# One core, eight sublayers: the dispatch multiply of a soft mixture of experts, and the square and key copies of an attention, change engines

## The chip, the core and the metric

The program runs on one core of a Trainium2 chip. The core has five engines that run their own instruction queues in order: PE (TensorE), DVE (VectorE), ACT (ScalarE), POOL (GpSimd) and SP (SyncE, which here only starts DMAs). They meet through semaphores. The metric is the device time of one launch in microseconds; the kernel before was run three times, and the profiled execution is the fastest of them.

## The reference

Eight sublayers over a residual stream `x` of 16 x 256 tokens of 128 numbers, each `x = x + layernorm(f(layernorm(x)))`. The change touches two of them. The soft mixture of experts, with 64 experts of 32 slots:

```
logits = einsum('bmd,dnp->bmnp', x, phi)        # b 16, m 256, 64*32 slots
dispatch = softmax(logits, axis=0)              # over the batches
combine = softmax(logits over all slots)
slots = einsum('bmd,bmnp->bnpd', x, dispatch)
y = einsum('bnpd,nde->bnpe', slots, W) + b
out = einsum('bnpd,bmnp->bmd', y, combine)
```

and the attention at the end of the seventh sublayer, with 16 query heads and 4 key heads of 8 numbers:

```
q, k, v = n @ q_w, n @ k_w, n @ v_w             # 128 + 32 + 32 columns
q, k = rms_norm(q), rms_norm(k)                 # per head, over 8 numbers
q, k = rope(q) * q_gain, rope(k)
k, v = repeat(k, 4), repeat(v, 4)               # a key head for 4 query heads
```

## The kernel before

All intermediate data stay in SBUF; the program goes from sublayer to sublayer. Each engine has a program of its own, made of Python generators; `together` advances the generators of several lanes in rounds, lane n one or more rounds behind lane n-1, so the order of an engine's queue is that of the rounds.

**Soft mixture of experts.** The 2048 slots go in 16 passes ("halves" `h` in the code) of 128 slots. The tokens of a batch are two tiles of 128, `mt` 0 and 1. For each pass and tile, `L3` holds the logits as 128 partitions by 16 batches by 128 slots (2048 columns) and `D3` the dispatch weights of the same shape. Two chains of buffers alternate. In one call of `dve_half`, DVE works on the fronts of pass h and finishes pass h-1:

- `dve_front(mt)`: the maximum over the batches by a tree of tensor_tensor instructions of 1024, 512 and 256 columns (L2051) and a last one (L2054), then the subtraction (L2064), the maximum over slots (L2065) and small updates.
- `dve_weights(mt)`: after ACT's exponential (L1966), the sum over the batches by the same tree, its reciprocal `m1` (L2083), and for tile 0 the multiply of `D3` by `m1` (L2086), 128x2048. This is the dispatch weight.
- then, for pass h-1, `dve_ya` four times (L2107: adds an expert product in psum to the output in SBUF) with `dve_eT3` between (L306: a copy from psum).

For tile 1 the same multiply is POOL's (`pool_half`, L2137), followed in its queue by the small sums `ls` (L2143, L2145). PE uses the product in `pe_slots` of the next half. PE's order is: logits of tile 1, slots, transposes and experts, then the products `pe_po` (L1929) with transposes and the next logits (L1870) between. ACT copies from psum (L302), takes the exponentials (L1966, L1975) and hands on the transposed outputs that the first L1929 of a half waits for; these copies stand in its queue behind the exponential of tile 1.

**Last attention.** 8 groups of 512 tokens in two runs of 4 lanes, one round apart. In each lane PE makes 192 columns of query, key and value for each token (L1262), ACT scales them out of psum into `QK` (L1712, L1713) and squares the 640 columns of queries and keys (L1718), DVE sums over each head (L1617), ACT takes the root of the mean plus epsilon (L1721), DVE inverts (L1620), applies the gain (L1623), scales (L1628) and turns by the position (L1636 to L1640). POOL writes each key head four times into `KR` (L1760, four copies of 128x128). PE transposes queries and then `KR` (`pe_tr4`, L294), DVE makes the masked queries from psum (L1562), ACT the masked keys (L1568). PE's attention matmuls (L389 and on) stand behind the last lane's transposes in its queue.

Of the kernel before, what the change touches and what calls it, by code (L numbers as in the profile page):

```python
# [10 lines left out]
ALU = mybir.AluOpType  # L11
# [6 lines left out]
LANES = 4  # L18
# [142 lines left out]
def build(nc, tables, wa, wb, wc, wd, wm, wi, ve, co, step, frame, xin, out):  # L161
    ctx = ExitStack()
    with ctx:
# [39 lines left out]

        ident = wv("ident")
        XG = [XA[:, 4 * g:4 * g + 4, :] for g in range(8)]
        mhalf, mone, epsc = MISC[:, 0:4], MISC[:, 212:216], MISC[:, 216:217]
        WI_S = wCs[:, 0:1152].bitcast(I32)
        WGU = wCs[:, 1152:2304]
        STEPM = wCs[:, 2304:2688]
# [134 lines left out]
        def idle(n):  # L344
            for _ in range(n):
                yield
# [861 lines left out]
        def pe_mid(pe, c, g):  # L1208
            v = views23(c)
            XT = v["XT"]  # L1210
            k = (("l2", g // 4), c.n)
            pe.wait_ge(A4, (("l2", g // 4), 2 * c.n + 1, "on"))
            pe_tok(pe, c, k, wv("l2o"), XT, 0, c.A, "y")
            pe.wait_ge(GD[LANES], "folded")
            yield
            yield
            k = (g, "l2f")
            pe.wait_ge(c.D, (k, "normed", 3))
            pe_tr4(pe, c, k, v["XN"], 0, c.A)
            yield  # L1220
            pe.wait_ge(c.A, (k, "xT"))
            yield from pe_mlp(pe, c, k, XT, wv("l2w1"), 4, w3("l2w2"), v["h3"], c.D, c.A)
            yield
            yield
            k = (g, "l3m")
            pe.wait_ge(c.D, (k, "mixed"))
            pe_tr4(pe, c, k, v["Z"], 0, c.A)
            yield
            k = (g, "l3n")
            pe.wait_ge(c.D, (k, "normed", 3))  # L1230
            pe_tr4(pe, c, k, v["YN"], 1, c.A)
            yield
            pe.wait_ge(c.A, (k, "xT"))
            pe.wait_ge(AD[LANES], "taps")
            for n in range(2):
                ps = c.bank(pe, n, c.A, (k, "val_silu", n))
                pe.e.matmul(ps[:, :], tap_weights(3, n), v["NT"], start=True, stop=False)
                for s in (1, 2, 3):
                    for b in range(0, 512, 256):
                        ins = pe.e.matmul(ps[:, b + s:b + 256], tap_weights(3 - s, n), v["NT"][:, b:b + 256 - s],  # L1240
                                          start=False, stop=s == 3 and b == 256)
                ins.then_inc(*c.P.inc((k, "val", n)))
            yield
            for n in range(2):
                ps = c.bank(pe, n, c.A, (k, "gated", n))
                pe.e.matmul(ps[:, :], wv("inp")[:, 256 + 128 * n:384 + 128 * n], v["NT"], start=True, stop=True).then_inc(
                    *c.P.inc((k, "gate", n)))
            yield
            for b in range(2):
                yield from pe_scan(pe, c, (g, "scan", b), b, v, (g, "l3n"), (g, "l3m"))  # L1250
            yield from pe_relu_mlp(pe, c, (g, "mm"), v, "mfc", "mpj")
            yield
            k = (("l3", g // 4), c.n)
            pe.wait_ge(c.D, ((g, "am"), "mixed"))
            pe_tr4(pe, c, k, v["Z"], 0, c.A)
            yield
            pe.wait_ge(c.A, (k, "xT"))
            for g2 in range(2):
                ps = c.bank(pe, g2, c.A, (k, g2, "qkv"))
                for j in range(2):  # L1260
                    t = 2 * g2 + j
                    ins = pe.e.matmul(ps[:, j * 192:(j + 1) * 192], XT[:, t * 128:(t + 1) * 128], wv("qkv"),  # L1262
                                      start=True, stop=True)
                ins.then_inc(*c.P.inc((k, g2, "qkv_pe")))
            yield
            yield
            yield
            pe.wait_ge(c.D, (k, "roped"))
            pe_tr4(pe, c, k, v["QK"][:, :, 0:128], 0, c.D, "qa")
            pe.wait_ge(c.G, (k, "repeated"))  # L1270
            pe_tr4(pe, c, k, v["KR"], 1, c.A, "ka")
            yield

# [307 lines left out]
        def dve_mid(dve, c, g):  # L1581
# [31 lines left out]
            yield  # L1613
            yield
            rb, sq, un = v["rb"], v["sq"], v["un"]
            dve.wait_ge(c.A, (k, "qk_sq"))
            dve.e.tensor_reduce(rb, sq.rearrange("p t (h d) -> p (t h) d", d=8), X_AX, ALU.add).then_inc(*c.D.inc((k, "ms")))  # L1617
            yield
            dve.wait_ge(c.A, (k, "rms"))
            dve.e.reciprocal(rb, rb).then_inc(*c.D.inc())  # L1620
# [16 lines left out]
            dve.e.tensor_tensor(u8[:, :, :, 0:4], q8[:, :, :, 4:8], turn("sin8", 0, 4), ALU.mult)  # L1637
            dve.e.tensor_tensor(u8[:, :, :, 4:8], q8[:, :, :, 0:4], turn("sin8", 4, 4), ALU.mult).then_inc(*c.D.inc())
            dve.wait_ge(c.D)
            dve.e.tensor_tensor(QK, sq, un, ALU.add).then_inc(*c.D.inc((k, "roped")))  # L1640
            yield
            dve_queries(dve, c, k, v, "mq", "qa_tr")
            yield
# [24 lines left out]
        def act_mid(act, c, g):  # L1668
# [45 lines left out]
                        "p (j d) -> p j d", d=8).unsqueeze(2).to_broadcast([128, 4, 4, 8]), ACT.Identity, scale=rs)  # L1714
                ins.then_inc(*c.A.inc((k, g2, "qkv")))
            ended([c.A], (k, "vp"))
            act.wait_ge(c.A, (k, 1, "qkv"))
            act.e.activation(v["sq"], QK, ACT.Square).then_inc(*c.A.inc((k, "qk_sq")))  # L1718
            yield
            act.wait_ge(c.D, (k, "ms"))  # L1720
            act.e.activation(v["rb"], v["rb"], ACT.Sqrt, scale=0.125, bias=epsc).then_inc(*c.A.inc((k, "rms")))  # L1721
            yield
            yield
            act_keys(act, c, k, v, "mk", "ka_tr")
# [13 lines left out]
        def pool_mid(pool, c, g):  # L1738
            yield from pool_norm(pool, c, (g, "l2ap"))
            yield from pool_norm(pool, c, (g, "l2f"))  # L1740
            yield from idle(3)
            yield from pool_norm(pool, c, (g, "l2fp"))
            yield from pool_norm(pool, c, (g, "l3x"))
            pool_mean_square(pool, c, (g, "l3n"), mhalf)
            yield
            v = views23(c)
            yield from idle(3)
            for b in range(2):
                yield from pool_scan(pool, c, (g, "scan", b), b, v, (g, "l3n"))
            pool_mean_square(pool, c, (g, "mm"), mone)  # L1750
            yield from idle(3)
            k = (("l3", g // 4), c.n)
            yield
            pool_mean_square(pool, c, k, mhalf)
            yield from idle(3)
            pool.wait_ge(c.D, (k, "roped"))
            for t in range(4):
                kr4 = v["KR"][:, t, :].rearrange("p (g r d) -> p g r d", g=4, d=8)
                k3_ = v["QK"][:, t, 128:160].rearrange("p (g d) -> p g d", d=8)
                ins = pool.e.tensor_copy(kr4, k3_.unsqueeze(2).to_broadcast([128, 4, 4, 8]))  # L1760
            ins.then_inc(*c.G.inc((k, "repeated")))
            yield from idle(2)

        def pool_fold(pool):

# [108 lines left out]
        def pe_slots(pe, banks, c, q):  # L1874
            k = ("smoe", q)
            for mt in range(2):
                D3 = views2(c, mt)["D3"]
                if mt == 0:
                    pe.wait_ge(c.D, (k, "disp"))
                else:  # L1880
                    pe.wait_ge(c.G, (k, 1, "disp"))
                for g in range(4):
                    if mt == 0:
                        banks.fill(pe, g, c.A, (k, "SL", g))
                    for i in range(4):
                        ins = pe.e.matmul(psum[g][:, i * 128:(i + 1) * 128], XN4[:, 4 * g + i, mt, :], D3[:, 4 * g + i, :],
                                          start=mt == 0 and i == 0, stop=mt == 1 and i == 3)
                    if mt == 1:
                        ins.then_inc(*c.P.inc((k, "slots", g)))
# [166 lines left out]
        def dve_front(dve, c, other, q, mt):  # L2056
# [1 line left out]
            tm, al, mr, m1 = v["tm"], v["al"], MR[:, mt, :], v["m1"]  # L2058
            dve.wait_ge(c.A, (k, mt, "L", 3))
            if q:  # L2060
                dve.wait_ge(other.G, (before, 1, "disp")) if mt else dve.wait_ge(other.D, (before, "disp"))
            dve_over_batches(dve, c, v["L3"], v["D3"], m1, ALU.max)
            dve.wait_ge(c.D)
            dve.e.tensor_tensor(v["D3"], v["L3"], v["mb"], ALU.subtract).then_inc(*c.D.inc((k, mt, "D")))  # L2064
# [13 lines left out]
        def dve_weights(dve, c, q, mt):  # L2078
            k, v = ("smoe", q), views2(c, mt)
            dve.wait_ge(c.A, (k, mt, "Dexp"))  # L2080
            dve_over_batches(dve, c, v["D3"], v["SL"], v["m1"], ALU.add)
            dve.wait_ge(c.D)
            dve.e.reciprocal(v["m1"], v["m1"]).then_inc(*c.D.inc((k, mt, "m1")))  # L2083
            if mt == 0:
                dve.wait_ge(c.D, (k, mt, "m1"))
                dve.e.tensor_tensor(v["D3"][:, 0:16, :], v["D3"][:, 0:16, :], v["mb"][:, 0:16, :],  # L2086
                                    ALU.mult).then_inc(*c.D.inc((k, "disp")))

        def dve_eT3(dve, c, q):
            for n in range(2):  # L2090
# [41 lines left out]

        def pool_half(pool, cs, h):
            c, other, k = cs[h % 2], cs[(h - 1) % 2], ("smoe", h)
            v = views2(c, 1)
            pool.wait_ge(c.D, (k, 1, "m1"))
            pool.e.tensor_tensor(v["D3"], v["D3"], v["mb"], ALU.mult).then_inc(*c.G.inc((k, 1, "disp")))  # L2137
            for mt in range(2):
                v, ls = views2(c, mt), LS[:, mt, :]
                pool.wait_ge(c.A, (k, mt, "E"))  # L2140
# [390 lines left out]

        def dve_program(e):
            dve = Engine(e)
            dve.e.memset(epsc, EPS).then_inc(*DD[LANES].inc("epsc"))
            dve.e.memset(mone, -1.0).then_inc(*DD[LANES].inc("mone"))
            dve.e.memset(mhalf, -0.5).then_inc(*DD[LANES].inc("mhalf"))
            dve.wait_dma(got_wi)
# [286 lines left out]
```

## Time and profile before

| | us |
|---|---|
| three runs, median (lowest, highest) | 3416.62 (3413.53, 3418.79) |
| the profiled execution, its own time | 3413.53 |
| its span in the trace | 3411.4 |
| PE busy, of the span | 2832.5 (83%) |
| DVE busy | 2209.4 (65%) |
| ACT busy | 1850.9 (54%) |
| POOL busy | 406.3 (12%) |
| mean granted clock of PE | 0.913 of full |
| the 16 passes of the mixture of experts, about | 1190 to 1820 |
| end of the two runs of query and key work | 2298 and 2930 |

The span is the time between the first and the last instruction of the program. Busy time is not time on the path that sets the end: only the chain of waits and the idle times, stretch by stretch, tell that.

### The profile page before, as it was taken

The numbers are of one execution on the slowest core, as the hardware profiler recorded it, in microseconds if no ns is written. First come the engines' busy times: TensorE is split into PE (matmuls) and PEld (weight loads), VectorE is DVE, ScalarE is ACT, GpSimd is POOL, SyncE is SP. The second block draws the span as 40 slices with busy tenths as digits, with TensorE's granted clock in tenths as the row PEclk, the third lists the DMA queues.
The fourth block names the chain that finished last, engine by engine and source line by source line (L and its number), as shares of the span: only waits on it lengthen the run. The fifth ranks groups of instructions, "written<-read, shape, count | busy, mean of one in ns | idle before, by whom it ended". The sixth has DMA issues, their size and how long they took to land.

```text
span 3411.4 us, 75794 instructions
## 1 busy us (share of the span) xinstructions
PE 2832.5 (83%) x31896; PEld 2260.7 (66%) x31896; DVE 2209.4 (65%) x5927; ACT 1850.9 (54%) x4115; POOL 406.3 (12%) x551
## 2 busy tenths in 40 slices
PE   5788888788888668888886889978887999786995
PEld 3566666556666568777785767867666787675574
DVE  4766656676656589899996663476565545755437
ACT  3566665566666578878783443354444434543332
POOL 1210101210001111111111011120100211002000
PEclk7899999899989889999997999988999999797997
DMA  2000000000000000000001000010100001001000
GB/s 96 1 2 1 2 1 1 1 1 2 14 1 14 29 7 7 7 7 7 7 1 63 3 14 13 1 50 3 39 15 3 25 2 38 14 3 50 1 1 26
DMA packets 16996, 48.95 MB, mean 14 GB/s; under 512 B 1168, under 2 KB 9616, under 8 KB 14096
## 3 DMA queue, kind: packets, MB, share of 16 engines
q1 hardware_dynamic: 16656, 44.10, 3.7%
q8 instruction: 252, 4.13, 0.5%
q14 instruction: 88, 0.72, 0.1%
HBM read 41.99 MB, written 2.10 MB: 13 GB/s over the span
## 4 chain that ended last, share of the span: by engine, by line
PE 54%; DVE 32%; ACT 10%; issue 2%; POOL 1%; DMA 0%; DVEq 0%; SPq 0%; POOLq 0%; ACTq 0%
PE ps L329 8%; PE ps L320 5%; PE ps L1358 3%; DVE LN L2051 3%; PE ps L1929 3%; PE ps L386 3%; PE ps L473 3%; DVE M L489 2%; DVE RS L239 2%; DVE LN L2064 2%; PE ps L1369 2%; PE ps L294 2%; PE ps L1870 2%; PE ps L754 2%; DVE M L633 1%
## 5 line engine op out<-in xcount | busy, mean ns | idle before, releaser
L302 ACT COPY LN<-ps 128x512 f32<-128x512 f32 (+4 forms) x560 | 284.9, 550 | 265.8 <-PE ps L772 59.5
L281 POOL TENSOR_TENSOR RS<-RS,MISC 128x4 f32<-128x4 f32 x184 | 189.1, 1028 | 1458.8 <-DVE RS L263 779.4
L489 DVE TENSOR_REDUCE M<-ps 128x6 f32<-128x768 f32 x256 | 241.6, 954 | 135.8 <-PE ps L473 95.5
L294 PE MATMUL ps<-cons,LN 128*128 128x128 f32 x672 | 125.3, 322 | 155.5 <-ACT LN L268 57.0
L386 PE MATMUL ps<-LN 32*128 32x256 f32 x1024 | 186.3, 438 | 55.2 <-DVE LN L525 31.6
L294 PEld LDWEIGHTS ps<-cons,LN 128*128 128x128 f32 x672 | 88.5, 163 | 200.0 <-ACT LN L268 55.0
L320 PE MATMUL ps<-LN,wAB 128*128 128x512 f32 x384 | 202.2, 658 | 19.4 <-DVE LN L959 18.1
L633 DVE TENSOR_REDUCE M<-ps 128x12 f32<-128x1536 f32 x64 | 112.4, 1756 | 146.5 <-PE ps L376 146.5
L389 PE MATMUL ps<-LN 32*128 32x256 f32 x1024 | 201.8, 473 | 2.2 <-DVE M L489 2.2
L1975 ACT ACTIVATE LN<-LN,RS 128x128 f32<-128x128 f32 x512 | 199.0, 404 | 1.6 <-DVE RS L2076 0.6
L549 ACT ACTIVATE LN<-ps 128x768 f32<-128x768 f32 x128 | 103.7, 810 | 168.2 <-PE ps L473 133.7
L329 PE MATMUL ps<-wAB,LN 128*128 128x128 f32 x1536 | 185.9, 280 | 7.1 <-DVE LN L1517 5.2
L329 PEld LDWEIGHTS ps<-wAB,LN 128*128 128x128 f32 x1536 | 179.4, 195 | 17.7 <-DVE LN L1517 9.1
L1929 PE MATMUL ps<-LN,wAB 128*128 128x128 f32 x1024 | 136.8, 291 | 44.1 <-ACT LN L302 43.6
L2051 DVE TENSOR_TENSOR LN<-LN 128x1024 f32<-128x1024 f32 (+2 forms) x192 | 150.7, 785 | 26.8 <-ACT LN L302 16.1
L539 ACT ACTIVATE LN<-ps 128x768 f32<-128x768 f32 x128 | 103.8, 811 | 112.9 <-PE ps L376 94.0
L1929 PEld LDWEIGHTS ps<-LN,wAB 128*128 128x128 f32 x1024 | 129.5, 205 | 48.0 <-ACT LN L302 47.1
L268 ACT ACTIVATE LN<-LN,RS 128x128 f32<-128x128 f32 x256 | 105.5, 488 | 76.4 <-POOL RS L275 75.3
L1870 PE MATMUL ps<-wAB,LN 128*128 128x128 f32 x1024 | 126.2, 281 | 22.3 <-ACT LN L302 21.0
L386 PEld LDWEIGHTS ps<-LN 32*128 32x128 f32 x1024 | 82.5, 190 | 92.1 <-issue 39.0
L1870 PEld LDWEIGHTS ps<-wAB,LN 128*128 128x128 f32 x1024 | 122.4, 198 | 22.8 <-ACT LN L302 21.2
L376 PE MATMUL ps<-cons 32*128 32x64 bf16 x6144 | 135.4, 193 | 0.3
(362 smaller groups left out, 7321.3 us busy)
## 6 DMA issues: line engine op xcount, KB each, us to landing
LN<-frame SPq DMA_DIRECT2D x16, 1024.0 KB, 5.0
wAB<-wb SPq DMA_DIRECT2D x16, 256.0 KB, 2.6
LN<-frame SPq DMA_DIRECT2D x8, 512.0 KB, 3.6
LN<-wd SPq DMA_DIRECT2D x8, 512.0 KB, 6.9
wAB<-wa SPq DMA_DIRECT2D x1, 3840.0 KB, 15.9
wCs<-wc SPq DMA_DIRECT2D x1, 2336.0 KB, 8.3
XA<-xin SPq DMA_DIRECT2D x8, 256.0 KB, 7.6
y<-XA SPq DMA_DIRECT2D x8, 256.0 KB, 2.3
```

What stands on the lines that cost most here:

```text
L281: pool.e.tensor_tensor(c.r[:, 40:44], c.r[:, 36:40], mhalf, ALU.pow).then_inc(*c.G.inc((k, "rstd")))
L294: ins = pe.e.transpose(ps[:, n * 128:(n + 1) * 128], src[:, n, :], ident)
L302: act.e.copy(dst, ps).then_inc(*c.A.inc(named(k, done)))
L320: pe.e.matmul(ps[:, :], w1[:, j * 128:(j + 1) * 128], xT, start=True, stop=True).then_inc(*c.P.inc((k, "up", j)))
L329: ins = pe.e.matmul(ps[:, t * 128:(t + 1) * 128], h3[:, j, t * 128:(t + 1) * 128], w2[:, j, :], start=j == 0, stop=j == nh - 1)
L386: pe.e.matmul(psum[n][:, 0:256], qt.ka[rows[j], o:o + 128], qt.qa[rows[j], o:o + 256], start=True, stop=False)
L389: pe.e.matmul(psum[n][:, 128:384], qs.qa[rows[j], o + 128:o + 256], qs.ka[rows[j], o:o + 256], start=True, stop=False)
L489: return dve.e.tensor_reduce(cols[:, 2 - 2 * h:4 - 2 * h, :, q.at], src, X_AX, ALU.max, negate=True)
L1870: ins = pe.e.matmul(psum[4 + g][:, i * 128:(i + 1) * 128], XTA[:, t * 128:(t + 1) * 128], phi[:, q * 128:(q + 1) * 128], start=True, stop= ...
L1929: ins = pe.e.matmul(psum[2 * gp + n][:, i * 128:(i + 1) * 128], eTb[2 * gp + n][:, i * 128:(i + 1) * 128], v["ym"][:, 4 * g + i, :], start ...
L1975: ins = act.e.activation(v["L3"][:, b, :], v["L3"][:, b, :], ACT.Exp, bias=v["nm"][:, b:b + 1], accum_out=v["rs"][:, b:b + 1])
L2051: dve.e.tensor_tensor(dst, src[:, 0:n, :], src[:, n:2 * n, :], op).then_inc(*c.D.inc())
```

## The change

In the mixture of experts, DVE's multiply for tile 0 goes to POOL: POOL's queue now has both multiplies of a pass, each released by the reciprocal of its tile, ahead of the `ls` sums. PE and DVE wait for POOL's count in place of DVE's. In the last attention, ACT's square becomes a DVE tensor_tensor, the factor 1/8 and epsilon move from ACT's square root into a DVE tensor_scalar ahead of it, and POOL's four copies of the keys become DVE copies behind the turn; the event "roped" comes after them, so the transposes of the queries wait for the copies too. The constant `epsc` and its memset go.

```diff
@@ pe_mid
             pe.wait_ge(c.D, (k, "roped"))
             pe_tr4(pe, c, k, v["QK"][:, :, 0:128], 0, c.D, "qa")
-            pe.wait_ge(c.G, (k, "repeated"))
             pe_tr4(pe, c, k, v["KR"], 1, c.A, "ka")
@@ dve_mid
-            dve.wait_ge(c.A, (k, "qk_sq"))
-            dve.e.tensor_reduce(rb, sq.rearrange(...), X_AX, ALU.add).then_inc(*c.D.inc((k, "ms")))
+            dve.wait_ge(c.A, (k, 1, "qkv"))
+            dve.e.tensor_tensor(sq, QK, QK, ALU.mult).then_inc(*c.D.inc())
+            dve.wait_ge(c.D)
+            dve.e.tensor_reduce(rb, sq.rearrange(...), X_AX, ALU.add).then_inc(*c.D.inc())
+            dve.wait_ge(c.D)
+            dve.e.tensor_scalar(rb, rb, 0.125, EPS, ALU.mult, ALU.add).then_inc(*c.D.inc((k, "ms")))
...
-            dve.e.tensor_tensor(QK, sq, un, ALU.add).then_inc(*c.D.inc((k, "roped")))
+            dve.e.tensor_tensor(QK, sq, un, ALU.add).then_inc(*c.D.inc())
+            dve.wait_ge(c.D)
+            for t in range(4):
+                kr4 = v["KR"][:, t, :].rearrange("p (g r d) -> p g r d", g=4, d=8)
+                k3_ = QK[:, t, 128:160].rearrange("p (g d) -> p g d", d=8)
+                ins = dve.e.tensor_copy(kr4, k3_.unsqueeze(2).to_broadcast([128, 4, 4, 8]))
+            ins.then_inc(*c.D.inc((k, "roped")))
@@ act_mid
-            act.wait_ge(c.A, (k, 1, "qkv"))
-            act.e.activation(v["sq"], QK, ACT.Square).then_inc(*c.A.inc((k, "qk_sq")))
...
-            act.e.activation(v["rb"], v["rb"], ACT.Sqrt, scale=0.125, bias=epsc).then_inc(*c.A.inc((k, "rms")))
+            act.e.activation(v["rb"], v["rb"], ACT.Sqrt).then_inc(*c.A.inc((k, "rms")))
@@ pool_mid: the wait for "roped" and the four tensor_copy into KR go
@@ pe_slots
-                if mt == 0:
-                    pe.wait_ge(c.D, (k, "disp"))
-                else:
-                    pe.wait_ge(c.G, (k, 1, "disp"))
+                pe.wait_ge(c.G, (k, mt, "disp"))
@@ dve_front
-                dve.wait_ge(other.G, (before, 1, "disp")) if mt else dve.wait_ge(other.D, (before, "disp"))
+                dve.wait_ge(other.G, (before, mt, "disp"))
@@ dve_weights
             dve.e.reciprocal(v["m1"], v["m1"]).then_inc(*c.D.inc((k, mt, "m1")))
-            if mt == 0:
-                dve.wait_ge(c.D, (k, mt, "m1"))
-                dve.e.tensor_tensor(v["D3"][:, 0:16, :], v["D3"][:, 0:16, :], v["mb"][:, 0:16, :],
-                                    ALU.mult).then_inc(*c.D.inc((k, "disp")))
@@ pool_half
-            v = views2(c, 1)
-            pool.wait_ge(c.D, (k, 1, "m1"))
-            pool.e.tensor_tensor(v["D3"], v["D3"], v["mb"], ALU.mult).then_inc(*c.G.inc((k, 1, "disp")))
+            for mt in range(2):
+                v = views2(c, mt)
+                pool.wait_ge(c.D, (k, mt, "m1"))
+                pool.e.tensor_tensor(v["D3"], v["D3"], v["mb"], ALU.mult).then_inc(*c.G.inc((k, mt, "disp")))
```

## Rows read from the trace of the kernel before

**Rows 1.** The page, part 1: busy us, share of the span, instructions.

```profile
PE 2832.5 (83%) x31896; PEld 2260.7 (66%) x31896; DVE 2209.4 (65%) x5927; ACT 1850.9 (54%) x4115; POOL 406.3 (12%) x551
```

**Rows 2.** The chain of waits from 1180 to 1850 us, shares by line.

```profile
by line: DVE LN L2051 16.8%; PE ps L1929 15.8%; DVE LN L2064 10.6%; PE ps L1870 8.4%; DVE LN L2086 5.5%; DVE RS L2065 4.9%; ACT LN L1966 4.9%; ACT LN L1975 4.4%; PE ps L1899 3.3%; DVE LN L2107 2.9%; ACT LN L302 2.5%; DVE M L2083 2.3%; issue
```

**Rows 3.** The two multiplies by line: ns least/median/most, first and last start.

```profile
L2086 DVE TENSOR_TENSOR LN<-LN,M x16: 2291/2292/2293, 1201.9 to 1767.1; 128x2048 f32<-128x2048 f32 x16
...
L2137 POOL TENSOR_TENSOR LN<-LN,M x16: 4535/4562/4580, 1215.7 to 1781.4; 128x2048 f32<-128x2048 f32 x16
```

**Rows 4.** Timeline of one half: start us, us, instruction, [idle before <-releaser].

```profile
1691.88 2.29 DVE L2086 TENSOR_TENSOR LN<-LN,M 128x2048 f32<-128x2048 f32 x1
...
1694.27 2.41 DVE L2051 TENSOR_TENSOR LN<-LN 128x1024 f32<-128x1024 f32 x3
...
1699.36 1.91 ACT L1966 ACTIVATE LN<-LN 128x2048 f32<-128x2048 f32 x1 [3.21 <-DVE LN L2064]
...
1702.77 2.83 PE L1929 MATMUL ps<-LN,wAB 128*128 128x128 f32 x16 [3.73 <-ACT LN L302]
...
1705.11 0.95 DVE L2083 RECIPROCAL M<-M 128x128 f32<-128x128 f32 x1
...
1706.14 4.58 POOL L2137 TENSOR_TENSOR LN<-LN,M 128x2048 f32<-128x2048 f32 x1 [23.27 <-DVE M L2083]
```

**Rows 5.** Timeline, instructions by line and chain where DVE and POOL overlap.

```profile
1215.74 4.54 POOL L2137 TENSOR_TENSOR LN<-LN,M 128x2048 f32<-128x2048 f32 x1 [36.23 <-DVE M L2083]
...
L2051 DVE TENSOR_TENSOR LN<-LN x1: 2064/2064/2064, 1219.3 to 1219.3; 128x1024 f32<-128x1024 f32 x1
...
1694.27 1.24 DVE LN L2051
...
1259.97 2.29 DVE L2064 TENSOR_TENSOR LN<-LN,M 128x2048 f32<-128x2048 f32 x1
1260.19 2.15 POOL L2145 TENSOR_TENSOR MISC<-MISC,RS 128x16 f32<-128x16 f32 x1
...
L2145 POOL TENSOR_TENSOR MISC<-MISC,RS x30: 218/222/2145, 1251.1 to 1791.6; 128x16 f32<-128x16 f32 x30
```

**Rows 6.** Chain at two halves; busy us by engine in one stretch, then PE's granted clock.

```profile
1552.68 2.05 PE ps L1929 x16
...
1557.39 1.79 PE ps L1870 x16
...
1709.13 1.79 PE ps L1870 x16
...
1702.70:1709.00 6.30, 6.23 (x41) 6.23 (x42) 5.92 (x16) 6.30 (x27) 2.86 (x1) 0.73 0.01 3
```

**Rows 7.** Last attention: PE, PEld, DVE, ACT, POOL busy by stretch; timeline, first run.

```profile
2273.00:2298.20 25.20, 9.91 (x36) 7.29 (x36) 22.78 (x38) 16.57 (x42) 4.99 (x15) 0.59 0.04 15
2905.30:2930.50 25.20, 9.77 (x36) 7.29 (x37) 22.77 (x38) 16.57 (x42) 4.99 (x15) 0.64 0.04 17
...
2269.92 1.13 DVE L1525 SCALAR_TENSOR_TENSOR LN<-ps,RS,LN 128x128 f32<-128x128 f32 x4 [3.35 <-PE ps L329]
...
2276.48 0.82 DVE L1640 TENSOR_TENSOR LN<-wAB,LN 128x640 f32<-128x640 f32 x1
...
2278.52 1.41 DVE L1562 TENSOR_SCALAR LN<-ps,cons 128x512 f32<-128x512 f32 x2 [0.48 <-PE ps L294]
...
2285.72 1.41 DVE L1562 TENSOR_SCALAR LN<-ps,cons 128x512 f32<-128x512 f32 x2 [0.86 <-PE ps L294]
...
2298.20 2.18 PE L294 MATMUL ps<-cons,LN 128*128 128x128 f32 x8 [4.63 <-DVE LN L1640]
2298.21 1.00 POOL L1760 COPY LN<-LN 128x128 f32<-128x128 f32 x4 [5.81 <-DVE LN L1640]
```

**Rows 8.** Groups of instructions by form: count, busy us, mean ns, idle before.

```profile
L824 DVE TENSOR_SCALAR LN<-LN 128x256 f32<-128x256 f32 x32 | 8.9, 278 | 0.0
...
L2075 DVE COPY MISC<-RS 128x16 f32<-128x16 f32 x32 | 5.6, 175 | 1.1
```

More of the change, by code:

```diff
@@ L205, in build @@
         XG = [XA[:, 4 * g:4 * g + 4, :] for g in range(8)]
-        mhalf, mone, epsc = MISC[:, 0:4], MISC[:, 212:216], MISC[:, 216:217]
+        mhalf, mone = MISC[:, 0:4], MISC[:, 212:216]
         WI_S = wCs[:, 0:1152].bitcast(I32)
@@ L1615, in dve_mid @@
             rb, sq, un = v["rb"], v["sq"], v["un"]
-            dve.wait_ge(c.A, (k, "qk_sq"))
-            dve.e.tensor_reduce(rb, sq.rearrange("p t (h d) -> p (t h) d", d=8), X_AX, ALU.add).then_inc(*c.D.inc((k, "ms")))
+            dve.wait_ge(c.A, (k, 1, "qkv"))
+            dve.e.tensor_tensor(sq, QK, QK, ALU.mult).then_inc(*c.D.inc())
+            dve.wait_ge(c.D)
+            dve.e.tensor_reduce(rb, sq.rearrange("p t (h d) -> p (t h) d", d=8), X_AX, ALU.add).then_inc(*c.D.inc())
+            dve.wait_ge(c.D)
+            dve.e.tensor_scalar(rb, rb, 0.125, EPS, ALU.mult, ALU.add).then_inc(*c.D.inc((k, "ms")))
             yield
@@ L1754, in pool_mid @@
             pool_mean_square(pool, c, k, mhalf)
[L1755 to L1762, printed above, removed]
+            yield from idle(5)
         def pool_fold(pool):
@@ L2533, in dve_program @@
             dve = Engine(e)
-            dve.e.memset(epsc, EPS).then_inc(*DD[LANES].inc("epsc"))
             dve.e.memset(mone, -1.0).then_inc(*DD[LANES].inc("mone"))
```

## The prediction

> **What bounds the kernel now.** I read the page first for the engines' shares, then the chain of waits over the soft mixture-of-experts stretch (1180 to 1850 us), where two thirds of the edits' instructions lie, then the timeline of one half of that stretch and of the end of the last attention's preparation, and last every place where a POOL instruction and a DVE instruction with two SBUF inputs overlap. The reader is to see four things.
>
> The page [rows 1] shows PE at 83% and DVE at 65% of the span, and says nothing of which one sets the end of a stage. The chain does: in the mixture-of-experts stretch the largest part is DVE's halving tree L2051, and L2086, the multiply that the change moves, holds 5.5% of it [rows 2]; 5.5% of 670 us is 36.9 us, which is all 16 instructions of 2.29 us [rows 3]. So each of the 16 halves waits for this multiply. The timeline says why [rows 4]: behind it on DVE stands the second tile's tree (L2051) and subtraction, and for that ACT (idle 3.21 us) and then PE (idle 3.73 us) wait.
>
> POOL is almost empty (12%) [rows 1], and does the same multiply for the second tile in 4.56 us [rows 3]. While it does so there, DVE works on psum (the `ya` updates and the `eT` copies), not on two SBUF tensors.
>
> **The mixture of experts, part by part (16 halves).** Removed from DVE: L2086. From its start to the start of the next L2051 are 1694.27 - 1691.88 = 2.39 us [rows 4]. The next L2051 now follows the reciprocal with the gap that it had behind L2086, 0.09 us, so the plain gain on the chain is 2.30 us in each half, 36.8 us in all. ACT and PE idle longer than that at this place, so nothing else would eat it.
>
> Added to POOL: one 4.56 us multiply per half, released by the same reciprocal. POOL starts such a multiply 0.08 us after the reciprocal ends (1705.11 + 0.95 against 1706.14) [rows 4]. DVE's L2051 comes 0.09 us after it. The two therefore start together in every half, both reading two SBUF tensors, which in the kernel before happens at no half but by accident once. That accident is what I go by [rows 5]: POOL's multiply ran from 1215.74 to 1220.28, L2051 started at 1219.30 inside it and took 2.06 us instead of 1.24. It ended at 1221.36, so its 1.24 us of work fit behind 1220.12: it stood still for 0.82 of the 0.98 us that the two shared, until 0.16 us before POOL's end. The reverse is there too: POOL's 16-column L2145, 0.22 us as a rule, began 0.22 us into DVE's L2064 and lasted 2.15 us, until 0.08 us after L2064 was done. An instruction of one engine holds up the other's for as long as it reads.
>
> The Trainium skill states this as a rule (SBUF — State Buffer, section "Who interferes with whom"): a DVE instruction with two SBUF inputs and a GpSimd instruction that reads SBUF exclude each other for the whole instruction, and the first to start decides who waits. By it the multiply would block for all of its 4.56 us, an estimate of 0.15 us a half, or 2.4 us in all, above what I take from the rows; it is the rule that speaks against this change. The trace agrees with it but for those last 0.16 us: 0.82 of 0.98 us lost [rows 5].
>
> With the rows: reciprocal ends at 1691.84, POOL starts at 1691.92, has read out 4.56 - 0.16 = 4.40 us later at 1696.32, and only then does L2051 run, which before started at 1694.27. That is 2.05 us later instead of 2.30 earlier. If DVE is the first by a hair, its 1024-column L2051 (1.24 us) runs, POOL's multiply goes next in the gap behind it, and the 512-column one waits: 0.09 + 1.24 + 4.4 = 5.73 us after the reciprocal against 0.04 + 2.39 + 1.24 = 3.67 before, again 2.06. Who wins doesn't matter. L2051 is on the chain in all 16 halves, so 16 x 2.05 = **33 us later**. Bounds: if the loser still creeps (0.16 us of work in 0.98 us of overlap) it does 0.7 us of its work meanwhile and the loss is 1.3 us a half, 21 us; if POOL holds to its very end and starts first, 2.2 us, 35.
>
> What waits for POOL is covered: PE needs both products only for the slot matmuls in the next half, and the front of the next half needs them later still. Behind the new multiply in POOL's queue stand the second multiply, whose reciprocal comes 13 us later, and the small `ls` updates. No DMA and no queue issue is moved.
>
> Clock of PE: PE idles 3.73 us ahead of the first product matmuls (L1929). From that start to the next logits are 1557.39 - 1552.68 = 4.71 us in one half, and 1709.13 - 1702.77 = 6.36 us in the half of [rows 4], where the same instructions fall partly under a granted clock of 1.2 GHz (mean share 0.73) [rows 4, 6]. Along the chain seven halves look like the first and the rest like the second or worse. The idle time grows to 5.8 us, which does not speak for a better clock. I take +3 us in all; bounds 0 and seven halves turned, 7 x 1.65 = 12.
>
> **The last attention's queries and keys, 4 lanes in each of two runs.** ACT loses one pass over 640 columns a lane; DVE gains a product of 128x640 (nearest row L1640, 0.82 us), a small scale-and-add on 80 columns and four copies of 128x128. Nearest rows for these: a copy of 16 columns takes 0.175 us, a tensor_scalar of 256 columns 0.278 [rows 8]; I take 0.19 for the small one with its wait and 0.20 for a copy, 0.83 for the four with their wait (0.6 to 1.2 as bounds). POOL loses the four copies, 1.00 us.
>
> From 2273.0 to 2298.2 DVE is busy for 22.78 of 25.2 us, the second run likewise [rows 7]: turning of lane 0, sum of lane 1, queries of lane 0, turning of lane 1, and so on. PE's transposes wait for the last DVE turn (L1640), and the attention's first matmuls stand behind those in PE's queue. So what DVE is given here is on the path, and what ACT gives up isn't: in the new order DVE is late and ACT waits for it. Four turnings gain 0.83 each, 3.3 us. Three sums gain 0.82 + 0.04 + 0.19 = 1.05 each, 3.15 us; the first lane's comes before DVE's idle stretch of 3.35 us, where it waits for PE [rows 7], and costs nothing. Against that, DVE has idle gaps for PE ahead of three of the queries (0.48, 0.86 and 0.48 us again; the first two in [rows 7]), which the added work fills: 1.8 us. POOL's copies ran beside the transposes of the queries (1.00 us beside 2.18 us, both from 2298.20) so their removal saves nothing at the end. 3.3 + 3.15 - 1.8 = 4.65 us a run, **9.3 us** for both; with the bounds of the copies 7.5 to 12, and 6 if half of the sums find more cover. If the cover of the three gaps is gone it is 13.
>
> The removed memset and the scale and bias of the square root change nothing that can be seen.
>
> **Sum.** 33 + 9.3 + 3 = 45.3 us, against the profiled execution's 3413.5 us (span 3411.4 and 2.1 around it): 3458.8. That execution is the fastest of three and 3.1 us under their median, so 3462 for a median.
>
> **Rivals.** (a) DVE keeps ahead. If L2051 gets the port first and its followers, 0.02 us apart, keep it, or if the block is a thing of the one overlap, POOL's multiply runs in the shadow and the 36.8 us are gained: 3416.6 - 36.8 + 9.3 = 3389 us. The point from which this decides is a stall of L2051 under 1.7 us a half ((36.8 - 9.3) / 16). For it: DVE's gaps are 0.02 us, and only one L2051 was seen waiting. Against it: L2145 got in right behind L2064 although DVE had more to do. 1 in 10.
> (b) The port is shared rather than locked, or the creeping of [rows 5] holds: 21 + 9.3 = 30 us, 3447; or the attention's part is hidden and only the stall counts, 33 us, 3450. 1 in 7, and inside the range.
> (c) The clock falls in the seven good halves as well, and copies cost 0.3 us each: 35 + 13 + 12 = 60 us, 3477. 1 in 14.
> (d) Everything cancels: a stall of some 1.7 us. 1 in 50.
>
> **How the numbers follow.** The forecast has two chances in three; with (b) and (c) 88 in 100 end slower. Its own range is 3452 to 3472; with the bounds and with (b) and (c) 3438 to 3482, which leaves out (a), (d) and a little more. What a measurement can tell from no change here is 0.2%, 7 us. Faster 0.10, same 0.02, slower 0.88.
>
> **What would show it.** In the profile after, every POOL multiply of the first tile begins within 0.1 us of a reciprocal; the L2051 beside it (1024 or 512 columns) takes 4.4 us longer than elsewhere; halves are 2 us longer each; ACT's and PE's idle time ahead of the exponential and of L1929 grows by 2 us. In the attention, DVE from 2273 on takes some 5 us more until the last turn. Wrong would be: L2051 at its 1.24 us (then rival a, and the multiply on POOL would show the wait or none at all); stalls in which each takes part of the other's time; or attention halves that end when they did.

## The result and the profile after

The median went from 3417.7 us (3413.53 to 3426.17, 4 runs) to 3473.0 us (3470.69 to 3478.71, 4 runs): a ratio of 1.0166, 95% interval 1.0149 to 1.0183, so 55.3 us slower. The forecast was 3462 within 3438 to 3482, slower. The profiled execution took 3474.84 us, with a span of 3473.0, 61.6 us more than the span before.

The page, part 1, of the kernel after:

```profile
span 3473.0 us, 75794 instructions
PE 2850.8 (82%) x31896; PEld 2280.3 (66%) x31896; DVE 2255.4 (65%) x5958; ACT 1846.9 (53%) x4107; POOL 473.9 (14%) x535
```

Against [rows 1], DVE gave away 16 multiplies of 2.29 us, 36.7 us, and is busy 46.0 us longer, although the attention gave it under 14 us of new instructions. An instruction that stands still counts as busy, so that is the first sign of a stall. PE is busy 18.3 us longer with as many instructions, at a mean granted clock of 0.905 where it was 0.913.

All rows below are of the kernel after unless said otherwise. Its line numbers are lower than before's: the tree is L2048 (was L2051), the subtraction L2061 (L2064), the reciprocal L2080 (L2083), POOL's multiply L2131 (L2137), the exponential L1963 (L1966), the products L1926 (L1929).

The timeline of one half, start us, us, instruction, idle before and its releaser (before: [rows 4]):

```profile
1736.29 4.55 POOL L2131 TENSOR_TENSOR LN<-LN,M 128x2048 f32<-128x2048 f32 x1 [9.11 <-DVE M L2080]
1736.31 6.78 DVE L2048 TENSOR_TENSOR LN<-LN 128x1024 f32<-128x1024 f32 x3
...
1745.78 1.91 ACT L1963 ACTIVATE LN<-LN 128x2048 f32<-128x2048 f32 x1 [5.26 <-DVE LN L2061]
...
1749.19 3.78 PE L1926 MATMUL ps<-LN,wAB 128*128 128x128 f32 x16 [5.77 <-ACT LN L302]
```

POOL and DVE leave the reciprocal together. POOL's multiply takes its usual time and the three tree instructions take 6.78 us instead of 2.41. ACT now idles 5.26 us ahead of the exponential instead of 3.21, and PE 5.77 us ahead of the products instead of 3.73: 2.05 and 2.04 us more.

The chain of waits through the same half, in order of time, and then the busy times of that stretch by engine with PE's granted clock behind them (before: [rows 6]):

```profile
1736.31 5.61 DVE LN L2048
...
1745.78 1.91 ACT LN L1963
...
1749.19 3.78 PE ps L1926 x16
1752.97 1.71 PE ps L1896 x8
1754.68 2.09 PE ps L1926 x16
1756.77 1.34 PE ps L1870 x12
...
1749.20:1756.80 7.60, 7.60 (x42) 7.60 (x43) 6.00 (x17) 7.48 (x33) 4.25 (x1) 0.61 0.01 2
```

The stalled tree instruction is on the chain, with 5.61 us. And the 40 matmuls and transposes from the first products to the next logits take 1756.77 - 1749.19 = 7.58 us, where [rows 6] has 4.71 in a good half and the prediction 6.36 in a bad one. The granted clock of that stretch was 0.61, so most of it ran at 1.2 GHz, and PE had idled 5.77 us before it.

The subtraction by line, ns least/median/most, first and last start; the tree's 1024-column form and the products by form, busy us, mean ns of one, idle us before. First after:

```profile
L2061 DVE TENSOR_TENSOR LN<-LN,M x32: 2291/2292/2293, 1196.8 to 1825.3; 128x2048 f32<-128x2048 f32 x32
...
L2048 DVE TENSOR_TENSOR LN<-LN 128x1024 f32<-128x1024 f32 x64 | 144.6, 2259 | 22.6 <-ACT LN L302 16.1 <-ACT LN L1963 0.8
...
L1926 PE MATMUL ps<-LN,wAB 128*128 128x128 f32 x1024 | 151.2, 310 | 74.9 <-ACT LN L302 74.4 <-DVE wAB L306 0.5
```

and the same of the kernel before:

```profile
L2064 DVE TENSOR_TENSOR LN<-LN,M x32: 2291/2292/2294, 1193.2 to 1772.3; 128x2048 f32<-128x2048 f32 x32
...
L2051 DVE TENSOR_TENSOR LN<-LN 128x1024 f32<-128x1024 f32 x64 | 79.2, 1238 | 22.4 <-ACT LN L302 16.1 <-ACT LN L1966 0.8
...
L1929 PE MATMUL ps<-LN,wAB 128*128 128x128 f32 x1024 | 136.8, 291 | 44.1 <-ACT LN L302 43.6 <-DVE wAB L306 0.5
```

The tree's 64 large instructions take 65.4 us more; that is 15 of them at 5.60 us (the sixteenth collision fell otherwise, below). From the first subtraction to the last the mixture of experts takes 628.5 us instead of 579.1. The two stretches start 3.6 us apart already. That start differs by up to 6.7 us between the traces of this document, although nothing of either edit but a memset lies before it, so it is not put to the change.

To see where in a half the time went I cut each one at four events and added up over the halves in each trace (us; 16 intervals in the first column, 15 in the next two, 14 in the last):

| kernel | subtraction of tile 0 to that of tile 1 | to the first products | first to third products | to the next subtraction |
|---|---|---|---|---|
| before | 227.7 | 86.0 | 109.2 | 152.0 |
| after | 260.2 | 86.0 | 127.3 | 152.3 |

All of it is in two places: 32.5 us in the interval that holds the stall, and 18.1 us in the stretch from the first products to the third, which is PE alone and where nothing was added. In single halves that stretch takes 6.34 us at full clock. Before, six of 15 halves had that and the rest mostly 7.98 (one 9.18); after, one half has 6.34 and nine have 8.7 to 9.3. The granted clock of the stretch goes with it: 1.00 at 6.34 us, 0.79 at 7.98, 0.67 to 0.68 at 9.2. The last half is shorter in every kernel: 6.20 before, 7.43 after, and 4.55 in experiment 4.

The attention, DVE in the first run (before: [rows 7]), with the first reciprocal and the first attention matmul as its marks:

```profile
2326.87 0.65 DVE L1623 RECIPROCAL wAB<-wAB 128x80 f32<-128x80 f32 x1
...
2331.19 0.63 DVE L1648 COPY LN<-LN 128x128 f32<-128x128 f32 x4
2331.74 0.82 DVE L1616 TENSOR_TENSOR wAB<-LN 128x640 f32<-128x640 f32 x1
...
2333.45 0.20 DVE L1620 TENSOR_SCALAR wAB<-wAB 128x80 f32<-128x80 f32 x1
...
2355.91 1.97 PE L294 MATMUL ps<-cons,LN 128*128 128x128 f32 x8 [6.04 <-DVE LN L1648]
...
2357.81 1.22 PE L389 MATMUL ps<-LN 32*128 32x256 f32 x4
```

and of the kernel before the same marks, with PE's wait for POOL's copies between them:

```profile
2273.02 0.65 DVE L1620 RECIPROCAL wAB<-wAB 128x80 f32<-128x80 f32 x1
...
2299.27 0.72 PEld L294 LDWEIGHTS ps<-cons,LN 128*128 128x128 f32 x4 [0.35 <-POOL LN L1760]
...
2300.32 1.22 PE L389 MATMUL ps<-LN 32*128 32x256 f32 x4
```

From mark to mark: 30.94 us after, 27.30 before, 3.64 us more; the second run gives 3.64 as well. Together 7.3 us. PE waits for DVE's copies now (6.04 us idle). The sum for the profiled execution is 32.5 + 18.1 + 7.3 = 57.9 us, and 3.6 from the later start: 61.5 of 61.6.

### The profile page after: what moved, and what is told of

Its sections match the earlier page's. It is cut to its first block, busy times and chain, and to the rows that moved or that the text cites. A ratio compares the mean times of both kernels' runs of the same rounds, so it can differ in the third digit from the quotient of the medians.

```text
span 3473.0 us, 75794 instructions
## 1 busy us (share of the span) xinstructions
PE 2850.8 (82%) x31896; PEld 2280.3 (66%) x31896; DVE 2255.4 (65%) x5958; ACT 1846.9 (53%) x4107; POOL 473.9 (14%) x535
## 4 chain that ended last, share of the span: by engine, by line
PE 54%; DVE 33%; ACT 9%; issue 2%; POOL 1%; DMA 0%; DVEq 0%; SPq 0%; POOLq 0%; ACTq 0%
PE ps L329 7%; DVE LN L2048 5%; PE ps L320 5%; PE ps L1926 3%; PE ps L1357 3%; PE ps L386 3%; PE ps L473 3%; DVE M L489 2%; DVE RS L239 2%; DVE LN L2061 2%; PE ps L1368 2%; PE ps L294 2%; PE ps L1870 2%; PE ps L754 2%; ACT LN L302 1%
## 5 line engine op out<-in xcount | busy, mean ns | idle before, releaser
L2048 DVE TENSOR_TENSOR LN<-LN 128x1024 f32<-128x1024 f32 (+2 forms) x192 | 220.3, 1147 | 27.0 <-ACT LN L302 16.1
L1926 PE MATMUL ps<-LN,wAB 128*128 128x128 f32 x1024 | 151.2, 310 | 74.9 <-ACT LN L302 74.4
L1926 PEld LDWEIGHTS ps<-LN,wAB 128*128 128x128 f32 x1024 | 143.9, 225 | 78.8 <-ACT LN L302 78.0
L2131 POOL TENSOR_TENSOR LN<-LN,M 128x2048 f32<-128x2048 f32 x32 | 146.3, 4570 | 356.5 <-DVE M L2080 356.5
L329 PEld LDWEIGHTS ps<-wAB,LN 128*128 128x128 f32 x1536 | 179.4, 195 | 17.7 <-DVE LN L1516 9.1
L2100 DVE SCALAR_TENSOR_TENSOR LN<-LN,RS,ps 128x128 f32<-128x128 f32 x448 | 119.1, 339 | 34.3 <-PE ps L1926 34.3
```

Source lines behind the costliest of these rows:

```text
L329: ins = pe.e.matmul(ps[:, t * 128:(t + 1) * 128], h3[:, j, t * 128:(t + 1) * 128], w2[:, j, :], start=j == 0, stop=j == nh - 1)
L1926: ins = pe.e.matmul(psum[2 * gp + n][:, i * 128:(i + 1) * 128], eTb[2 * gp + n][:, i * 128:(i + 1) * 128], v["ym"][:, 4 * g + i, :], start ...
L2048: dve.e.tensor_tensor(dst, src[:, 0:n, :], src[:, n:2 * n, :], op).then_inc(*c.D.inc())
```

## The experiments

**1. The mixture-of-experts edit alone.** The diff's hunks of `pe_slots`, `dve_front`, `dve_weights` and `pool_half`; the attention as before.

> Only the mixture-of-experts edit, the attention as before. My theory (POOL's reading multiply shuts DVE's two-SBUF instructions out, and the delay then lets PE's clock fall): the 16 halves keep all of their 50 us (16 x 2.05 stall, some 18 from the clock), so about 3467 us, ratio 1.015; the 1024-column tree instruction beside POOL's multiply takes 5.6 us. Rival (the two edits make each other worse): under 40 us.

Measured: 3461.5 us (3461.16 to 3466.98) against 3417.9, ratio 1.0131 (1.0117 to 1.0144), 43.6 us. A half in its timeline:

```profile
1610.15 4.55 POOL L2131 TENSOR_TENSOR LN<-LN,M 128x2048 f32<-128x2048 f32 x1 [9.05 <-DVE M L2080]
1610.18 6.80 DVE L2048 TENSOR_TENSOR LN<-LN 128x1024 f32<-128x1024 f32 x3
...
1623.07 3.78 PE L1926 MATMUL ps<-LN,wAB 128*128 128x128 f32 x16 [5.79 <-ACT LN L302]
```

The same stall and the same slow products as with the whole change: first to last subtraction 628.6 us against 579.1, so the stretch holds the 50 us that were expected, while the medians show 43.6. By the medians four fifths of the loss are this edit's.

**2. The attention edit alone.**

> Only the attention edit, the multiply on DVE as before. My theory: 3.7 to 3.9 us in each of the two runs of lanes, 7.5 us in all, ratio 1.0022, and nothing elsewhere. Rival (the 3.5 us that the changed kernel is already behind ahead of the mixture of experts belong to the edit): 11 us.

Measured: 3424.3 us (3416.06 to 3438.87, 10 runs), ratio 1.0020 (1.0005 to 1.0034), 6.5 us. Its marks:

```profile
2272.64 0.65 DVE L1623 RECIPROCAL wAB<-wAB 128x80 f32<-128x80 f32 x1
...
2303.58 1.22 PE L389 MATMUL ps<-LN 32*128 32x256 f32 x4
```

30.94 us, the same 3.64 us a run more as with the whole change. In the stretches the two edits add up; by the medians they make 43.6 + 6.5 = 50.1 of 55.3 us, with some 5 us of uncertainty in each.

**3. The delay without POOL.** The kernel before, with one more DVE instruction behind the multiply that lasts about as long as the net delay of a half, 2.05 us (its result is used nowhere):

```diff
                                     ALU.mult).then_inc(*c.D.inc((k, "disp")))
+                dve.wait_ge(c.D, (k, "disp"))
+                dve.e.tensor_tensor(v["SL"][:, 0:14, :], v["D3"][:, 0:14, :], v["D3"][:, 0:14, :],
+                                    ALU.add).then_inc(*c.D.inc())
```

> The kernel before with one more DVE instruction of 1792 columns behind the multiply of tile 0 (it adds two copies of data into a scratch buffer and changes no result): the same 2.05 us of delay in each half, with POOL left alone. If the rest of the loss is PE's clock, as I hold, the halves come out as in the changed kernel: about 50 us, the time from the first products to the third ones at 8.5 us on average instead of 7.4, all L2051 at 1.24 us. If instead POOL and DVE cost more in other places (rival), this kernel loses only 33 us.

Measured: 3471.6 us (3466.13 to 3476.23), ratio 1.0156 (1.0140 to 1.0171). One half, the subtraction by line and the products by form:

```profile
1618.05 2.03 DVE L2089 TENSOR_TENSOR LN<-LN 128x1792 f32<-128x1792 f32 x1
...
1620.18 2.41 DVE L2051 TENSOR_TENSOR LN<-LN 128x1024 f32<-128x1024 f32 x3
...
L2064 DVE TENSOR_TENSOR LN<-LN,M x32: 2291/2291/2296, 1199.2 to 1827.7; 128x2048 f32<-128x2048 f32 x32
...
L1929 PE MATMUL ps<-LN,wAB 128*128 128x128 f32 x1024 | 151.2, 311 | 74.8 <-ACT LN L302 74.3 <-DVE wAB L306 0.5
```

The tree takes its 2.41 us, POOL is left as it was, and the stretch is 628.5 us all the same, with the products at 311 ns and the first-to-third stretches adding up to 127.0 us. So the 18 us on PE come with the delay alone; they need nothing of POOL's. The medians of experiments 1 and 3 are 10 us apart although this stretch is the same to 0.1 us: in the profiles 5.5 us of that lie ahead of the mixture of experts (first subtraction at 1193.6 and 1199.2) and 3.5 behind it, where the two kernels do not differ. A difference of a few microseconds between medians of two kernels is not evidence here; the stretches are.

**4. POOL does both multiplies, but later.** Experiment 1 with the first multiply released by the second tile's reciprocal, when DVE goes on to instructions that read psum:

```diff
-                pool.wait_ge(c.D, (k, mt, "m1"))
+                pool.wait_ge(c.D, (k, 1, "m1"))
```

> The mixture-of-experts edit alone, but POOL begins both multiplies only after the second tile's reciprocal, when DVE works on psum for about 10 to 12 us; they take 9.1 us. My theory: no overlap with a two-SBUF instruction of DVE, every tree instruction of 1024 columns at 1.24 us, 2.3 us gained in each half, 37 us, and up to 15 more because PE's idle time falls to 1.4 us and its clock holds: 3365 to 3380 us, ratio 0.985 to 0.989. Rival 1 (POOL's load itself costs time, wherever it lies): no gain. Rival 2 (the multiplies run into the next half's tree): gain shrinks by the overlap, seen as tree instructions above 1.24 us.

Measured: 3373.6 us (3370.92 to 3376.86), ratio 0.9870 (0.9857 to 0.9884): 44.3 us faster than before, and 99 faster than the change, which has the attention's 7 us as well. A half of it, the granted clock of a stretch, and the subtraction by line:

```profile
1596.27 2.41 DVE L2048 TENSOR_TENSOR LN<-LN 128x1024 f32<-128x1024 f32 x3
...
1604.78 2.05 PE L1926 MATMUL ps<-LN,wAB 128*128 128x128 f32 x16 [1.40 <-ACT LN L302]
...
1608.15 9.09 POOL L2131 TENSOR_TENSOR LN<-LN,M 128x2048 f32<-128x2048 f32 x2 [20.95 <-DVE M L2080]
...
1604.80:1609.30 4.50, 4.50 (x40) 4.50 (x41) 4.36 (x11) 4.50 (x17) 1.15 (x1) 1.00 0.00 0
...
L2061 DVE TENSOR_TENSOR LN<-LN,M x32: 2291/2292/2294, 1194.7 to 1734.0; 128x2048 f32<-128x2048 f32 x32
```

The tree is not held up, PE idles 1.40 us, and the granted clock of the stretch behind it is 1.00, the level of 2.4 GHz. By the cuts of the table above: the first column falls by 37.1 us (the multiply off DVE's path, 16 x 2.30 = 36.8), the third by 16.0 (14 halves at 6.34, the last at 4.55), and the second grows by 6.9. That last growth is PE's clock too, at an earlier place:

```profile
1414.86 5.51 PE L1906 MATMUL ps<-LN,wAB 128*128 128x512 f32 x8 [5.66 <-ACT LN L302]
...
1424.39 2.05 PE L1926 MATMUL ps<-LN,wAB 128*128 128x128 f32 x16 [0.40 <-ACT LN L302]
```

In seven halves PE had idled 2.2 to 5.7 us ahead of the expert matmuls (L1906), which then took 5.2 to 6.6 us instead of the 3.67 of the other halves. PE came to the products with 0.4 us of idle time left and was itself late; those seven halves hold all of the 6.9 us.

The gain from taking the multiply off DVE was there to be had; it was the place of POOL's multiply beside the tree that cost more than it. In the first half, where DVE goes from the second reciprocal into another tree, they still collide: one tree instruction takes 5.49 us there.

**5. Half of POOL's reading.** Experiment 1 with the first tile's multiply over 8 of the 16 batches; the other 8 stay without the factor.

```diff
-                pool.e.tensor_tensor(v["D3"], v["D3"], v["mb"], ALU.mult).then_inc(*c.G.inc((k, mt, "disp")))
+                nb = 16 if mt else 8
+                pool.e.tensor_tensor(v["D3"][:, 0:nb, :], v["D3"][:, 0:nb, :], v["mb"][:, 0:nb, :],
+                                     ALU.mult).then_inc(*c.G.inc((k, mt, "disp")))
```

> As the mixture-of-experts edit alone, but POOL's multiply for tile 0 takes 8 of the 16 batches (1024 columns; the other 8 stay unscaled). My theory (DVE stands still for as long as POOL reads): POOL's instruction 2.3 us, the tree instruction beside it 1.24 + 2.1 = 3.4 us, its end 0.2 us a half earlier than before the change, time within 5 us of before. Rival (a fixed cost of each collision): 5.6 us as in the changed kernel.

Measured, one run each: 3418.3 us against 3420.6 for the kernel before. The timeline of one half:

```profile
1621.21 2.36 POOL L2132 TENSOR_TENSOR LN<-LN,M 128x1024 f32<-128x1024 f32 x1 [9.06 <-DVE M L2080]
1621.24 4.60 DVE L2048 TENSOR_TENSOR LN<-LN 128x1024 f32<-128x1024 f32 x3
```

The three tree instructions take 4.60 us, 2.19 more than undisturbed, beside an instruction of 2.36 us. The stall goes with how long POOL reads: 4.37 of 4.55 us in the half after, 2.19 of 2.36 here. The 1024-column instruction beside it takes 3.40 to 3.42 us, as expected (3.4). What is lost then nearly equals what DVE was spared (2.30 us): the first column of the table is 225.6 us, 2.1 under before.

**6. POOL writes and does not read.** Experiment 1 with the first tile's multiply replaced by a memset of the same buffer, so the dispatch weights of that tile are zero:

```diff
-                pool.e.tensor_tensor(v["D3"], v["D3"], v["mb"], ALU.mult).then_inc(*c.G.inc((k, mt, "disp")))
+                if mt:
+                    ins = pool.e.tensor_tensor(v["D3"], v["D3"], v["mb"], ALU.mult)
+                else:
+                    ins = pool.e.memset(v["D3"], 0.0)
+                ins.then_inc(*c.G.inc((k, mt, "disp")))
```

> As the mixture-of-experts edit alone, but in place of the multiply for tile 0 POOL sets those 2048 columns to zero (tile 0 gives no dispatch; nothing is read by POOL), about 2 us. If only reading shuts DVE's second input out: tree instruction 1.24 us, each half 2.3 us shorter than before, some 3370 us. If POOL and DVE exclude each other in any case (rival): tree instruction 3 us, time like before.

Measured, one run each: 3369.4 us against 3420.6 for the kernel before. The timeline of one half:

```profile
1625.80 1.80 POOL L2134 MEMSET LN<- 128x2048 f32 x1 [9.04 <-DVE M L2080]
1625.85 2.41 DVE L2048 TENSOR_TENSOR LN<-LN 128x1024 f32<-128x1024 f32 x3
```

POOL writes for 1.80 us beside the tree, and the tree takes its undisturbed 2.41. So writing alone does not shut DVE out; the multiply, which also reads, does. The Trainium skill says so too (SBUF — State Buffer, "Who interferes with whom": two SBUF inputs on DVE contend with a GpSimd instruction that reads SBUF, "not with one that only writes it"), and this trace agrees, with 2.41 us beside the memset and 6.80 beside the multiply. An instruction of POOL that only reads was not tried.

**7 and 8. The attention edit in two halves.** The kernel before with only the square moved to DVE (with the scale-and-add), and the kernel before with only the copies moved to DVE.

> Only the square and the scale-and-add move to DVE. My theory: three sums of 1.05 us more on the path of each run, of which DVE's gaps ahead of the queries take 1.8: 1.3 us a run, 2.6 us in all. Rival (the square was on ACT's path and moving it gains): end of the run no later than before.

> Only the four copies of the keys move to DVE. My theory: four times 0.68 us on the path of each run, with the gaps ahead of the queries left as they are: 2.7 us a run, 5.4 in all. Rival (POOL's copies had held the transposes up, so the move pays for itself): under 1 us a run.

Measured, one run each: 3415.1 and 3418.0 us against 3420.6. Whole runs can't tell 2 us apart here; the marks can. The square alone:

```profile
2274.18 0.64 DVE L1624 RECIPROCAL wAB<-wAB 128x80 f32<-128x80 f32 x1
...
2302.70 1.22 PE L389 MATMUL ps<-LN 32*128 32x256 f32 x4
```

and the copies alone:

```profile
2277.30 0.65 DVE L1619 RECIPROCAL wAB<-wAB 128x80 f32<-128x80 f32 x1
...
2306.65 1.22 PE L389 MATMUL ps<-LN 32*128 32x256 f32 x4
```

28.52 and 29.35 us against 27.30: 1.22 and 2.05 us a run, where 1.3 and 2.7 were expected. Their sum is 3.27 and together they cost 3.64, because both fill the same gaps of DVE: the copies alone shorten the gap of 0.86 us [rows 7] to 0.48, and the square alone takes all three. Together there are still only the 1.8 us to fill.

**9. The delay with PE kept busy.** Experiment 1, with one set of the transposes ahead of the idle stretch of PE done four times over, each time with the same values:

```diff
-                for i in range(4):
+                for i in range(4 * (1 + (3 if p == 2 else 0))):
+                    i = i % 4
```

> The mixture-of-experts edit alone, and PE does the third set of transposes of each half four times over instead of once (24 more of 128x128, the same results into the same banks), which fills some 3 of the 5.8 us that it idles ahead of the first products. The stall of DVE stays. If the idle time is what lets PE's clock fall (my theory), the time from the first to the third products comes back to 6.3 us in all halves and the halves cost 33 us less what the kernel before loses itself, so 3430 to 3440 us against 3461 without the idle work. If the clock falls for another reason (rival: the longer half, or DVE's and POOL's load), those 8.5 us and the 50 us stay or grow by PE's added work.

Measured: 3457.2 us (3448.81 to 3459.39), ratio 1.0116 (1.0098 to 1.0133): 4.3 us better than experiment 1 by the medians, where 20 and more were expected, and not told from it, since the intervals (1.0117 to 1.0144 there) overlap. The expectation was wrong by this measure. In the trace, one half and the products by form:

```profile
1649.86 3.66 PE L1897 MATMUL ps<-cons,LN 128*128 128x128 f32 x32
...
1656.67 2.77 PE L1927 MATMUL ps<-LN,wAB 128*128 128x128 f32 x16 [3.15 <-ACT LN L302]
...
L1927 PE MATMUL ps<-LN,wAB 128*128 128x128 f32 x1024 | 140.9, 297 | 38.5 <-ACT LN L302 38.0 <-DVE wAB L306 0.5
```

PE's idle time ahead of the products is halved (38.5 us in all, 74.9 after), and the first-to-third stretches add up to 113.4 us instead of 127.3: 13.9 of the 18.1 us are back, with DVE's stall left as it was. So idle time of PE does carry this term. Six halves are back at 6.34; in five of them PE idled only 0.9 to 1.6 us ahead of the products. It isn't the length alone: of the ten halves with 3.15 us one has 6.34, four have 9.06 to 9.14, and the rest 7.8 to 8.0 (the short last one 7.4). Less of the gain is seen in the medians than in this stretch; the start of the mixture of experts was 4.8 us later than in experiment 1's profile.

**10. The same transposes in the kernel before**, three times over instead of four.

> The kernel before, with the same transposes done three times over (16 more of each half), filling 2.1 of the 3.7 us of idle time. My theory: nine halves lose their 1.65 us and more, 15 to 18 us in all, ratio 0.995 to 0.996. Rival: no gain, or a loss where the added transposes push the first products.

Measured: 3412.4 us (3406.57 to 3421.36, 10 runs), ratio 0.9992 (0.9981 to 1.0003): not told from no change. The products by form:

```profile
L1930 PE MATMUL ps<-LN,wAB 128*128 128x128 f32 x1024 | 133.4, 287 | 20.7 <-ACT LN L302 18.9 <-DVE wAB L306 1.8
```

The first-to-third stretches add up to 101.2 us instead of 109.2, where 15 to 18 had been expected to go. Nine halves idle 2.0 us ahead of the products now instead of 3.7; four of them are at full clock and five still show 7.96 to 7.98.

## Why the prediction was right, and where its sum was off

**The stall, right to a few hundredths.** Predicted 2.05 us a half, 33 in all; measured 32.5 over the 16 intervals between the subtractions, 14.22 to 16.27 us in a typical one. The tree instruction takes 5.60 us where 1.24 + 4.4 was worked out. One overlap of 0.98 us [rows 5] gave that: it showed a full stop, and that the stop ends 0.16 us ahead of POOL's end. Experiment 5 shows what the prediction only argued, that the block lasts as long as POOL's instruction, and experiment 6 that an instruction which only writes makes none.

**"Who wins doesn't matter", right.** In the first half after, the timeline has DVE ahead by 0.14 us:

```profile
1205.44 6.58 DVE L2048 TENSOR_TENSOR LN<-LN 128x1024 f32<-128x1024 f32 x3
1205.58 5.44 POOL L2131 TENSOR_TENSOR LN<-LN,M 128x2048 f32<-128x2048 f32 x1 [22.52 <-DVE M L2080]
```

The 1024-column instruction ran in 1.22 us with POOL waiting, then POOL went in ahead of the 512-column one. That half is 1.85 us longer (13.73 to 15.58 between the subtractions) against 2.05 in the others. Rival (a), in which DVE keeps the port, needed DVE's instructions to hold POOL off across their 0.02 us gaps; POOL got in at the first of them. The prediction's ground against (a) was weak, though: what DVE had next when L2145 got in [rows 5] was a reduction (L2065) with a single SBUF input, so that row did not test whether DVE's next two-input instruction would have kept POOL out.

**The step that was mis-sized is the clock of PE:** "I take +3 us in all; bounds 0 and seven halves turned, 7 x 1.65 = 12." It measured 18.1 us. The place and the cause were the right ones (PE idles longer ahead of the products, and the same instructions then take longer), as experiments 3 and 9 show, one by making the loss without POOL and the other by giving most of it back without touching the stall. The 3 itself was worked out from no row, and its upper bound was too low because it let good halves turn bad but no bad half turn worse, at 6.36 - 4.71 = 1.65 us each [rows 6], although the prediction itself says "or worse". The worse case is 7.58 us at a granted clock of 0.61, and one half of the kernel before shows it as well: 9.18 us from the first to the third products. With six halves at 6.34, seven at 7.98 and a PE that idles 5.8 us instead of 3.7, the bound was some six times 9.2 - 6.34 and seven times 9.2 - 7.98, 26 us, and the estimate something well inside it. For the same reason the sign "halves are 2 us longer each" was too low: a half like that of [rows 4] went from 37.6 to 41.0 us.

The prediction also did not ask why some halves were good. In the kernel before these are the six in which PE had idled 2.2 to 5.7 us ahead of the expert matmuls (L1909):

```profile
1462.76 6.43 PE L1909 MATMUL ps<-LN,wAB 128*128 128x512 f32 x8 [4.97 <-ACT LN L302]
...
1473.78 2.05 PE L1929 MATMUL ps<-LN,wAB 128*128 128x128 f32 x16 [0.97 <-ACT LN L302]
```

There the expert matmuls take 5.3 to 6.4 us instead of 3.67 (granted clock 0.57 in the one shown), which uses up PE's idle time ahead of the products: 1.0 to 2.1 us are left, and the products run at 1.00. All nine other halves idle 3.7 us there, and none of them has its products at full clock. So a good half has paid the clock at another place, where PE had idle time to spare, and the 2.05 us more of idle time took that cover away in five of the six.

**The attention, 7.3 us for 9.3.** The path was the right one: DVE, with PE waiting for its last instruction. Three sizes were off. The four copies of a lane put DVE's next instruction 0.66 us later, not 0.83 (experiment 8's trace). The square and the scaling cost 1.01 us a lane, not 1.05 (experiment 7's). That the removal of POOL's copies "saves nothing at the end" was wrong: PE had waited 0.35 us for POOL's copies, and the last transposes take 1.97 us instead of 2.18, 0.21 less. That makes 4 x 0.17 + 3 x 0.04 + 0.21 = 1.0 us a run, and 4.65 - 3.64 is 1.0. The cover of 1.8 us by DVE's gaps was right.

**The sum.** 33 + 9.3 + 3 = 45.3 predicted; 32.5 + 7.3 + 18.1 = 57.9 in the trace, 55.3 between the medians. The forecast's own range (3452 to 3472) missed by 1 us, the wide one held because rival (c) had been let in. That the total came within 11 us of the forecast is in part luck: the clock's term was 15 us too small and the attention's 2 too large, and rival (c)'s 12 + 13 us for these two terms come to the 18.1 + 7.3 measured only because one is too low and the other too high.

**Left open.** What, besides the length of PE's idle time, decides which halves get the lower clock and for how long: after the change an idle time of 3.00 us stands before 9.27 us and one of 3.39 before 6.34, and the halves of experiments 9 and 10 with equal idle times differ as well. The 18 us are therefore shown to come from the delay and PE's longer idle time, but their size can't be derived from it.

## What to carry to other kernels

Before a DVE instruction is handed to POOL, look at what DVE does in the microseconds after the release: if that is a tensor_tensor with both inputs in SBUF, the move costs nearly the whole time of POOL's instruction on DVE (4.37 of 4.55 us here) and can be worse than no move, while the same work some microseconds later, beside DVE's reads of psum, cost DVE nothing in 15 of 16 halves (1.3% faster instead of 1.3% slower). A stall that lets PE idle longer is to be charged twice, once for itself and once for the clock behind it; here the second was over half of the first. How long a stretch of PE can become is read from all repetitions of the stage in the trace before, not from two of them, and a repetition that looks good is asked what it has paid elsewhere.

## What was not expected of the hardware

- A longer idle stretch of PE, 5.8 us instead of 3.7 in halves of some 41, cost 18 us in 15 halves, 1.2 us a half, though PE was idle for only some 1.5 us of the rest of such a half: granted clock 0.61 in the stretch behind it (0.73 in [rows 6], 1.00 in experiment 4 behind 1.40 us).
- POOL is not slowed by DVE when it comes first: its multiply of 128x2048 took 4.55 us beside the stalled tree and 4.56 elsewhere. With DVE first it took 5.44, 0.9 more, of the 1.08 us that it shared with DVE's instruction of 1.22.
- POOL's memset of 128x2048 (1.80 us) and DVE's tree (2.41 us for three) ran side by side with no loss to the tree.
